# A four-part kernel (attention, experts, delta rule, feed-forward): attention's maxima taken in pairs on TensorE's row halves, and the query and key parts moved as four-byte words

## The chip, the cores and the metric

One core of one Trainium2 chip. The metric is the device time of one execution in microseconds (us); three runs of the kernel before lie within 0.15% of each other.

## What is computed

The input x has 2048 tokens of 256 numbers. Four blocks follow each other, each as `x = x + layernorm(block(layernorm(x)))`; the change touches the first alone.

```python
# block 1: 16 heads of 16 numbers, float32
q = rope(x @ q_w.T + q_b); k = rope(x @ k_w.T + k_b); v = x @ v_w.T + v_b
probs = softmax(einsum('bhqd,bhkd->bhqk', q, k) * 16 ** -0.5)
out = einsum('bhqk,bhkd->bhqd', probs, v) @ out_w.T + out_b
# block 2: 16 experts of which 2 are chosen for each token, and a shared one
# block 3: gated delta rule, 32 value heads, a scan over 256 tokens
# block 4: feed-forward of width 1024 with quantised weights
```

## The kernel before

The phases run one behind the other, each a block of its own with a program for every engine: PE (TensorE), DVE (VectorE), ACT (ScalarE), POOL (GpSimd) and SP (the queue that issues DMAs). A phase begins when every engine has ended the one before. The order on each engine is the order in which the code is written; engines wait for each other by counters.

**Head phase** (`head_phase`, line 173). It normalises x, turns it, and projects queries and keys: 16 blocks `n` of 128 features (8 heads) by 512 tokens, in the order q, k, k, q of four blocks each (`place`). A block passes DVE (`rotate`, line 389), POOL (`put_together`), ACT (`highest`, line 350), DVE (`remainder`), ACT (`middle`) and POOL (`lowest`), and leaves three bfloat16 parts, high, middle and low, whose sum is the float32 value. SP writes the three parts of each block to DRAM (line 235, `parts_away`), and after each four blocks reads them back (line 243, `heads_back`) so that the 16 features of a head stand on partitions in six bands of 16 rows, in such an order that one product over the 96 rows adds the six part products that count. Such a load is three DMAs, of 48, 32 and 16 partitions with 32 KB each. All DMAs of SP go through one queue in order. `highest` of block n waits until the writes of block n - 3 have landed, since there are three buffers (`parts`). The values are projected last (line 323).

**Attention phase** (`attention_phase`, line 418). A step is one tile of 128 keys or queries of one head; there are 16 steps to a head, 256 in all. Softmax needs each query's maximum first:

- `maximum` (line 494) multiplies 128 queries by 512 keys with the 96 rows of the six bands, four times per step, into a ring of three PSUM banks `mx`; DVE takes the maximum of each (line 632). After a head's last step DVE splits the 16 x 128 maxima into three bfloat16 parts (`split_maxima`, lines 600 to 611), PE turns them (line 525), ACT copies them (line 580) and SP writes them as rows 96 to 98 of the query operand (line 590). The key operand has ones there, set once and copied in the head phase (lines 227 and 399), so that scores come out with the maximum taken off.
- `scores` (line 505): 99 rows, 128 keys by 512 queries, four per step, in two PSUM tiles `sc` of 1024. ACT takes the exponential of each 1024 (line 568).
- `weigh` (line 517): values by probabilities, in float32, the four blocks of queries on four groups of 32 columns of the array, into `o_ps`. A float32 matmul is two instructions in the trace.
- At a head's end ACT copies `o_ps` (line 574), PE turns it (line 534), and DVE divides (lines 620 and 623).

Scores run `LAG` = 20 steps behind the maxima. PE's order in a step is mx, two scores, mx, two scores, mx, o_ps of the step before, mx. POOL stages each head's values (line 475).

## Time and profile before

| | us |
|---|---|
| median of three runs | 3882.52 (3880.14 to 3885.17) |
| the profiled execution | 3883.3 |
| its span, first to last instruction | 3881.6 |
| head phase | 0 to 145.3 |
| attention: maxima alone | 145.3 to 195.7 |
| attention: steps with maxima and scores | 195.7 to 888 |
| attention: scores alone | 888 to 934.9 |
| the other three blocks | 934.9 to 3881.6 |

The trace is of one execution. A row of its time line has the start, the time from the first start to the last end, the engine, the line of the code, the operation with its tiles and shapes, and how many instructions it merges; in brackets the idle time before it and what ended that. PE's matmuls are pipelined and their ends are modelled, so what counts for PE is the distance between starts. PEld is the load of a matmul's weights, SPq an issue on SP's queue, PEq the sequencer of PE.

### The profile page before, as it was taken

What the parts mean: (1) busy time and instruction counts of PE and PEld (TensorE: products, weight loads), DVE (VectorE), ACT (ScalarE), POOL (GpSimd) and SP (SyncE); (2) the same over time, 40 slices, a digit from 0 to 9 for tenths busy, and PEclk for the clock granted to TensorE, in tenths of its full rate; (3) what the DMA queues carried; (4) which work ended last, traced back from release to release, by engine and by line L of the source; (5) the groups of instructions that cost most, each with busy time, mean ns of one, the idle gap of its engine ahead of it and who ended that gap; (6) DMA issues with size and microseconds to landing.
All of it is one profiled execution on the core that took longest, in us unless ns stands there. A gap on an engine that the chain in (4) does not pass through costs nothing. (4 is left out here: it accounts for less than half of the span.)

```text
span 3881.6 us, 69297 instructions
## 1 busy us (share of the span) xinstructions
PE 3555.1 (92%) x22894; PEld 2220.9 (57%) x22894; DVE 2831.3 (73%) x6720; ACT 2428.1 (63%) x6502; POOL 1926.0 (50%) x4662
## 2 busy tenths in 40 slices
PE   6699999998896379999999999999999999999789
PEld 3133333333553247777777777777777777777645
DVE  4688888883423368888888888888888888888543
ACT  1066666666232367777777777777777777777411
POOL 3100000001302267877777777777777787777300
PEclk9599999999898589999999999999999999999999
DMA  6500000003222111111111110111111111111010
GB/s 162 95 1 1 1 1 1 1 1 128 96 81 86 34 27 30 39 33 30 40 34 28 41 41 21 40 41 29 32 41 31 38 33 41 30 36 25 16 37 17
DMA packets 201619, 149.25 MB, mean 38 GB/s; under 512 B 148740, under 2 KB 185732, under 8 KB 197681
## 3 DMA queue, kind: packets, MB, share of 16 engines
q1 hardware_dynamic: 198192, 136.42, 13.7%
q0 software_dynamic: 3072, 8.39, 0.7%
q8 instruction: 187, 3.06, 0.3%
q14 instruction: 168, 1.37, 0.1%
HBM read 102.69 MB, written 41.68 MB: 37 GB/s over the span
## 5 line engine op out<-in xcount | busy, mean ns | idle before, releaser
L2260 POOL TENSOR_TENSOR dl_blocks_tmp<-dl_blocks_l,dl_blocks_x 128x60 f32<-128x60 f32 (+24 forms) x1984 | 713.1, 359 | 307.4 <-DMA dl_blocks_l<-lm_dram 171.4
L2265 POOL TENSOR_TENSOR dl_blocks_x<-dl_blocks_x,dl_blocks_tmp 128x60 f32<-128x60 f32 (+24 forms) x1984 | 701.7, 354 | 155.4
L632 DVE TENSOR_REDUCE part_max<-mx 128x1 f32<-128x512 f32 x1024 | 637.0, 683 | 81.4 <-PE mx L494 81.3
L568 ACT ACTIVATE normed_t<-sc 128x1024 f32<-128x1024 f32 x512 | 496.4, 1021 | 222.1 <-PE sc L505 221.9
L2417 DVE SCALAR_TENSOR_TENSOR dl_conv<-dl_raw,dl_weights,dl_conv 128x512 f32<-128x512 f32 x768 | 580.7, 784 | 28.5 <-ACT dl_conv L2188 23.9
L1959 PE MATMUL prep<-normed_t,dl_weights 128*128 128x512 f32 x1024 | 484.2, 596 | 18.7 <-DMA dl_weights<-in_w_delta 17.3
L494 PE MATMUL mx<-k_t,q_t 96*128 96x512 bf16 x1024 | 375.0, 401 | 23.9 <-PEq L182 15.1
L475 POOL COPY v_staged<-v 128x256 f32<-128x256 f32 x16 | 6.3, 400 | 704.6 <-PE o_ps L517 704.6
L2118 ACT ACTIVATE dl_q_state<-rec_a,t_neg_decay 128x128 f32<-128x128 f32 x512 | 160.4, 366 | 239.4 <-DVE dl_r L2322 239.4
L505 PE MATMUL sc<-q_t,k_t 99*128 99x512 bf16 x1024 | 305.5, 381 | 0.6
L2128 ACT ACTIVATE dl_v<-rec_b,dl_s 128x128 f32<-128x128 f32 x512 | 164.9, 385 | 175.8 <-DVE dl_v L2330 97.2
L517 PE MATMUL o_ps<-normed_t,v_staged 128*32 128x512 f32 x2048 | 272.7, 605 | 0.4 <-ACT normed_t L568 0.4
L2064 PE MATMUL gate_y_ps<-dl_weights,dl_gated_t 128*128 128x256 f32 x1024 | 271.7, 388 | 0.9 <-ACT dl_gated_t L2133 0.9
L494 PEld LDWEIGHTS mx<-k_t,q_t 96*128 96x128 bf16 x1024 | 82.8, 97 | 324.3 <-DVE part_max L632 253.8
L2330 DVE TENSOR_TENSOR dl_v<-rec_b,dl_s_decayed 128x256 f32<-128x256 f32 x256 | 108.7, 425 | 213.6 <-PE rec_b L2037 204.7
L1959 PEld LDWEIGHTS prep<-normed_t,dl_weights 128*128 128x128 f32 x1024 | 176.7, 192 | 148.0 <-issue 144.3
L1973 PE MATMUL prep<-dl_weights,normed_t 128*128 128x256 f32 x1024 | 249.5, 387 | 0.0
L2289 POOL TENSOR_TENSOR dl_out_scale<-dl_out_scale,t_mhalf 128x2 f32<-128x2 f32 x256 | 185.9, 726 | 82.3 <-ACT dl_out_scale L2143 65.6
L2187 ACT ACTIVATE dl_raw<-prep 128x512 f32<-128x512 f32 x256 | 153.1, 598 | 102.4 <-PE prep L1959 102.3
L2322 DVE SCALAR_TENSOR_TENSOR dl_r<-rec_a,t_neg_decay,dl_v_scaled 128x128 f32<-128x128 f32 x512 | 155.2, 344 | 83.2 <-PE rec_a L2028 81.2
L2338 DVE SCALAR_TENSOR_TENSOR dl_state<-dl_state,t_chunk_decay,rec_a 128x128 f32<-128x128 f32 x512 | 153.8, 341 | 71.7 <-PE rec_a L2044 69.7
L1973 PEld LDWEIGHTS prep<-dl_weights,normed_t 128*128 128x128 f32 x1024 | 185.2, 191 | 22.6
(306 smaller groups left out, 7810.0 us busy)
## 6 DMA issues: line engine op xcount, KB each, us to landing
dl_blocks_l<-lm_dram SPq DMA_DIRECT2D x256, 128.0 KB, 2.7
dl_weights<-in_w_delta SPq DMA_DIRECT2D x16, 1032.0 KB, 4.9
lm_dram<-dl_lm SPq DMA_DIRECT2D x256, 32.0 KB, 1.7
xs_dram<-dl_blocks_x SPq DMA_DIRECT2D x64, 128.0 KB, 2.5
dl_inverse_t<-xs_dram SPq DMA_DIRECT2D x256, 32.0 KB
qk_dram<-hd_parts SPq DMA_DIRECT2D x48, 128.0 KB
rows_dram<-moe_zeros SPq DMA_DIRECT2D x1, 6016.0 KB, 23.1
moe_x_rows<-rows_dram SPq DMA_DIRECT2D x47, 128.0 KB, 2.2
```

The costliest lines, as they stand in the source:

```text
L494: pe.matmul(bank_of(x)[:, :], QT[0:SPLIT_ROWS, i, qt * P:(qt + 1) * P], KT[0:SPLIT_ROWS, i, b * 512:(b + 1) * 512], start=True, stop=True) ...
L505: last = pe.matmul(sc[u][:, b, :], KT[0:SCORE_ROWS, h, kt * P:(kt + 1) * P], QT[0:SCORE_ROWS, h, (2 * u + b) * BQ:(2 * u + b + 1) * BQ], s ...
L517: last = pe.matmul(o_ps[32 * qb:32 * qb + 32, :], vs[h % 2][:, kt, :], probs[:, kt % 2, qb * BQ:(qb + 1) * BQ], start=(kt == 0), stop=(kt ...
L568: act.activation(probs[:, e % 2, u * 2 * BQ:(u + 1) * 2 * BQ], flat(sc[u][:, :, :]), ACT.Exp, scale=float(DH) ** -0.5).then_inc(s["exp_don ...
L632: dve.reduce_max(part_max[:, t % NT, x[2]:x[2] + 1], bank_of(x)[:, :], AX.X).then_inc(s["ring_read"], 1)
L1959: last = pe.matmul(flat(bank[:, :, :]), proj_w(kh, k, m, 1), x_cols(k, q, 0, QT_), start=(k == 0), stop=(k == KD - 1))
L1973: last = pe.matmul(flat(PB[1 + u][:, 2 * j:2 * j + 2, :]), x_cols(k, q, (2 * u + j) * P, P), proj_w(kh, k, CH, VH), start=(k == 0), stop=( ...
L2064: last = pe.matmul(gy[:, 1, :], gt[g % 2][:, h, :], w_out(kh)[:, h, :], start=(h == 0), stop=(h == VH - 1))
L2260: pool.tensor_tensor(out, L[:, 0:i, i].unsqueeze(1).broadcast_to([P, NM - c0, i]), Xs[:, c0:NM, i:i + 1].broadcast_to([P, NM - c0, i]), AL ...
L2265: pool.tensor_tensor(Xs[:, c0:NM, 0:i], Xs[:, c0:NM, 0:i], out, ALU.add).then_inc(s["solve_step"], 1)
L2289: pool.tensor_tensor(osc[g % 2][:, :], osc[g % 2][:, :], tab["mhalf"], ALU.pow).then_inc(s["root_done"], 1)
L2417: dve.scalar_tensor_tensor(cv[:, m, :], raw[:, m, k:k + QT_], tap(kh, m, k), cv[:, m, :], ALU.mult, ALU.add).then_inc(s["conv_step"], 1)
```

## The change

The layout of the six bands depends on the head's parity. An even head's operands stand on rows 0 to 95 with its maxima on rows 96 to 98; an odd head's bands are turned by 64 rows, to 64 to 127 and 32 to 63, with the maxima on rows 0 to 2 and zeros on 3 to 31. The four products that matter for a maximum now fill rows 0 to 63 of an even head and rows 64 to 127 of an odd one. In each step but the first and last eight, the two matmuls of a pair belong to neighbouring heads, the upper half of one's query tiles beside the lower half of the next one's; they write the two banks of one `mx` tile, which DVE reduces in one instruction. Both pairs of a step stand between scores two and three. The scores have three PSUM tiles of 512 and ACT takes exponentials of 512. The ring has two slots of two banks, the lag is 28 steps.

The parts go through DRAM as float32 words of two bfloat16 numbers; a load comes in six pieces (q) or eight (k) instead of three, for even and odd heads apart. The ones and zeros are set by POOL at the start of attention instead of by DVE and a DMA in the head phase.

On PE, some steps into attention; `mx0` to `mx2` and `sc0` to `sc2` are PSUM tiles, `o_ps` the weighted values. Before:

```order
L494 MATMUL mx2<-k_t,q_t 128x512
L494 MATMUL mx0<-k_t,q_t 128x512
L505 MATMUL sc0<-q_t,k_t 128x512 x2
L494 MATMUL mx1<-k_t,q_t 128x512
L505 MATMUL sc1<-q_t,k_t 128x512 x2
L494 MATMUL mx2<-k_t,q_t 128x512
L517 MATMUL o_ps<-normed_t,v_staged0 32x512 x4
```

The same place now:

```order
L557 MATMUL sc0<-q_t,k_t 128x512
L557 MATMUL sc1<-q_t,k_t 128x512
L545 MATMUL mx1<-k_t,q_t 128x512 x2
L545 MATMUL mx0<-k_t,q_t 128x512 x2
L557 MATMUL sc2<-q_t,k_t 128x512
L557 MATMUL sc0<-q_t,k_t 128x512
L569 MATMUL o_ps<-normed_t,v_staged0 32x512 x4
```

The four mx matmuls, which stood apart between the scores, stand together as two pairs, with scores on both sides.

On SP in the head phase, from the first part writes to the third load; `hd_parts` are the parts, `q_t` and `k_t` the operands. Before:

```order
L235 DMA qk_dram<-hd_parts 8x16x512 x15
L243 DMA q_t<-qk_dram 48x16384
L243 DMA q_t<-qk_dram 32x16384
L243 DMA q_t<-qk_dram 16x16384
L235 DMA qk_dram<-hd_parts 8x16x512 x12
L243 DMA k_t<-qk_dram 48x16384
L243 DMA k_t<-qk_dram 32x16384
L243 DMA k_t<-qk_dram 16x16384
L235 DMA qk_dram<-hd_parts 8x16x512 x12
```

And now:

```order
L238 DMA qk_dram<-hd_parts 8x16x256 x15
L250 DMA q_t<-qk_dram 32x4096 x6
L238 DMA qk_dram<-hd_parts 8x16x256 x12
L250 DMA k_t<-qk_dram 32x4096
L250 DMA k_t<-qk_dram 16x4096 x2
L250 DMA k_t<-qk_dram 32x4096 x2
L250 DMA k_t<-qk_dram 16x4096 x2
L250 DMA k_t<-qk_dram 32x4096
L238 DMA qk_dram<-hd_parts 8x16x256 x12
```

The places of the loads between the writes are the same; each load is six or eight issues of half the bytes per partition and at most 32 partitions.

```diff
+def place_of(h):
+    return h // 8 * 8 + h % 8 // 2 + h % 2 * 4
...
-    PART_AT = ((0, 1, 2), (2, 1, 0))
+    PART_AT = ((1, 2, 0), (1, 0, 2))
+    BANDS = (((0, 2, slice(1, 3)), (32, 2, slice(1, 3)), (64, 2, slice(0, 2))),
+             ((0, 2, slice(0, 2)), (32, 1, slice(1, 2)), (48, 1, slice(0, 1)), (64, 2, slice(1, 3))))
...
-            sp.wait_ge(s["one_set"], 1)
-            sp.dma_start(KT[SPLIT_ROWS:SCORE_ROWS, 1:HEADS, :],
-                         KT[SPLIT_ROWS:SCORE_ROWS, 0:1, :].broadcast_to([MAX_ROWS, HEADS - 1, T])
-                         ).then_inc(s["ones_in"], 16)
...
-                    sp.dma_start(a["qk_dram"][side, u, part, :, :, BT * b:BT * b + BT].rearrange("d h t -> h d t"),
-                                 parts[n % DEEP][:, part, :]).then_inc(parts_out[n % DEEP], 16)
+                    sp.dma_start(a["qk_dram"][side, u, part, :, :, BW * b:BW * b + BW].rearrange("d h t -> h d t"),
+                                 parts[n % DEEP][:, part, :].bitcast(F32)).then_inc(parts_out[n % DEEP], 16)
...
-                for band, first, n in ((0, 0, 3), (3, side, 2), (5, 2 * side, 1)):
-                    sp.dma_start(flat((QT, KT)[side][DH * band:DH * (band + n), HALF * u:HALF * u + HALF, :]),
-                                 a["qk_dram"][side, u, first:first + n, :, :, :].rearrange("c d h t -> (c d) (h t)")
-                                 ).then_inc(heads_in[u], 16)
+                for odd in range(2):
+                    for row, band, chosen in BANDS[side]:
+                        at = (row + 64 * odd) % P if row < 64 else 64 - 32 * odd
+                        quarter = slice(HALF // 2 * odd, HALF // 2 * (odd + 1))
+                        to = slice(HALF * u + quarter.start, HALF * u + quarter.stop)
+                        sp.dma_start((QT, KT)[side][at:at + DH * band, to, :].rearrange("p h t -> p (h t)").bitcast(F32),
+                                     a["qk_dram"][side, u, chosen, :, quarter, :].rearrange("c d h t -> (c d) (h t)")
+                                     ).then_inc(heads_in[u], 16)
...
-            dve.memset(KT[SPLIT_ROWS:SCORE_ROWS, 0, :], 1.0).then_inc(s["one_set"], 1)
...
-    LAG = NT + 4
-    RING = 3
+    HALF = NT // 2
+    LAG = NT + HALF + 4
+    RING = 2
+    LEAD = SPLIT_ROWS - 2 * DH
...
-        mx = [c.ps(ctx, f"mx{i}", [P, 512]) for i in range(RING)]
-        sc = [c.ps(ctx, f"sc{i}", [P, 2, 512]) for i in range(2)]
+        mx = [c.ps(ctx, f"mx{i}", [P, 2, 512]) for i in range(RING)]
+        sc = [c.ps(ctx, f"sc{i}", [P, 512]) for i in range(3)]
...
+        def pair(t, v):
+            if t < HALF or t >= STEPS - HALF:
+                h, q = (0, t) if t < HALF else (HEADS - 1, t - STEPS + NT)
+                return [(h, q, 2 * v), (h, q, 2 * v + 1)]
+            h, j = divmod(t - HALF, NT)
+            b = 2 * (j % 2) + v
+            return sorted([(h, HALF + j // 2, b), (h + 1, j // 2, b)], key=lambda x: x[0] % 2)
...
+            for h in range(HEADS):
+                if h % 2:
+                    pool.memset(QT[0:2 * DH, place_of(h), :], 0.0).then_inc(s["rows_set"], 1)
...
+                    pool.memset(KT[0:2 * DH, place_of(h), :], 0.0).then_inc(s["rows_set"], 1)
...
+                pool.memset(KT[at:at + MAX_ROWS, place_of(h), :], 1.0).then_inc(s["rows_set"], 1)
...
-                pe.matmul(bank_of(x)[:, :], QT[0:SPLIT_ROWS, i, qt * P:(qt + 1) * P],
-                          KT[0:SPLIT_ROWS, i, b * 512:(b + 1) * 512], start=True, stop=True
-                          ).then_inc(s["ring_filled"], 1)
+                for i, (h, q, b) in enumerate(pair(t, v)):
+                    at = 64 * (h % 2)
+                    last = pe.matmul(bank_of(x)[:, i, :], QT[at:at + LEAD, place_of(h), q * P:(q + 1) * P],
+                                     KT[at:at + LEAD, place_of(h), b * 512:(b + 1) * 512], start=True, stop=True)
+                last.then_inc(s["ring_filled"], 1)
...
-                if e:
-                    pe.wait_ge(s["exp_done"], 2 * (e - 1) + u + 1)
...
+                    pe.wait_ge(s["rows_set"], rows_set_by(h))
+                if n >= 3:
+                    pe.wait_ge(s["exp_done"], n - 2)
...
             for t in range(LAST):
                 e = t - LAG
+                if 0 <= e < STEPS:
+                    scores(e, 0)
+                    scores(e, 1)
                 if t < STEPS:
                     maximum(t, 0)
...
                     maximum(t, 1)
                 if 0 <= e < STEPS:
-                    scores(e, 1)
...
+                    scores(e, 2)
+                    scores(e, 3)
                 if 0 <= e - 1 < STEPS:
                     weigh(e - 1)
...
-                        dve.reduce_max(part_max[:, t % NT, x[2]:x[2] + 1], bank_of(x)[:, :], AX.X
-                                       ).then_inc(s["ring_read"], 1)
+                        low, high = ((h % 2) * NT * QB + q * QB + b for h, q, b in pair(t, x[2]))
+                        dve.tensor_reduce(flat(part_max[:, :, :, :])[:, low:high + 1:high - low], bank_of(x)[:, :, :],
+                                          AX.X, ALU.max).then_inc(s["ring_read"], 1)
...
-    aps["qk_dram"] = nc.dram_tensor("qk_dram", (2, 2, 3, DH, HEADS // 2, T), BF16).ap()
+    aps["qk_dram"] = nc.dram_tensor("qk_dram", (2, 2, 3, DH, HEADS // 2, T // 2), F32).ap()
```

The weights' columns are sorted to match `place_of` on the host side of the program's layout; the projections themselves, the values among them, are as before.

## Rows read from the trace of the kernel before

**Rows 1.** Busy us of each engine by stage, granted clock, DMA share.

```profile
core 0: us, PE busy (x) PEld busy (x) DVE busy (x) ACT busy (x) POOL busy (x), PEclk, DMA share, GB/s
145.30:195.70 50.40, 48.80 (x85) 8.97 (x86) 49.49 (x88) 0.27 (x1) 1.61 (x6) 0.50 0.35 53
195.70:888.00 692.30, 682.19 (x3835) 209.35 (x3832) 608.50 (x1055) 468.62 (x500) 5.60 (x14) 1.00 0.01 1
```

**Rows 2.** Time line of PE, a steady step: start, us, engine line op.

```profile
600.50 0.60 PE L494 MATMUL mx<-k_t,q_t 96*128 96x512 bf16 x2
600.94 0.60 PE L505 MATMUL sc<-q_t,k_t 99*128 99x512 bf16 x2
...
602.03 0.38 PE L494 MATMUL mx<-k_t,q_t 96*128 96x512 bf16 x1
602.34 1.06 PE L517 MATMUL o_ps<-normed_t,v_staged 128*32 128x512 f32 x8
603.34 0.39 PE L494 MATMUL mx<-k_t,q_t 96*128 96x512 bf16 x1
```

**Rows 3.** The same step, DVE and ACT; in brackets, idle time before.

```profile
600.93 2.48 DVE L632 TENSOR_REDUCE part_max<-mx 128x1 f32<-128x512 f32 x4 [0.35 <-PE mx L494]
601.58 1.94 ACT L568 ACTIVATE normed_t<-sc 128x1024 f32<-128x1024 f32 x2 [0.90 <-PE sc L505]
```

**Rows 4.** Time line of PE in the delta phase: matmuls on 32-row groups.

```profile
2513.26 0.69 PE L1994 MATMUL merge_ps<-dl_inverse_t,dl_lm 32*32 32x32 f32 x32
```

**Rows 5.** Time lines of PE, expert phase, narrow windows: 128 and 48 rows.

```profile
1032.49 0.38 PE L1050 MATMUL moe_y_ps<-moe_w_down,moe_hidden_t 128*128 128x256 f32 x1
1032.71 0.79 PE L1050 MATMUL moe_y_ps<-moe_w_down,moe_hidden_t 128*128 128x256 f32 x2
1033.02 0.70 PE L1050 MATMUL moe_y_ps<-moe_w_down,moe_hidden_t 48*128 48x256 f32 x2
1033.34 0.38 PE L1050 MATMUL moe_y_ps<-moe_w_down,moe_hidden_t 48*128 48x256 f32 x1
1033.64 0.56 PE L1019 MATMUL moe_gu_ps<-moe_w_gate_up,normed_t 128*128 128x352 f32 x1
```

**Rows 6.** DVE's reductions: one line's least/median/most ns; time line of the fill.

```profile
L632 DVE TENSOR_REDUCE part_max<-mx x1024: 671/681/694, 146.0 to 888.8; 128x1 f32<-128x512 f32 x171
145.97 38.35 DVE L632 TENSOR_REDUCE part_max<-mx 128x1 f32<-128x512 f32 x64 [0.52 <-PE mx L494]
184.36 0.22 DVE L600 TENSOR_REDUCE neg_max<-part_max 128x16 f32<-128x64 f32 x1
146.72 0.10 PEld L494 LDWEIGHTS mx<-k_t,q_t 96*128 96x128 bf16 x1 [0.84 <-DVE part_max L632]
```

**Rows 7.** ACT's copy of 128 x 512 out of PSUM: least/median/most ns.

```profile
L574 ACT ACTIVATE out_sb<-o_ps x16: 597/598/604, 245.4 to 932.6; 128x512 f32<-128x512 f32 x16
```

**Rows 8.** Time line of ACT in the tail: two steps.

```profile
927.51 3.90 ACT L568 ACTIVATE normed_t<-sc 128x1024 f32<-128x1024 f32 x4 [0.27 <-PE sc L505]
```

**Rows 9.** Head phase: issues, ACT, PE; DMA issues xcount, KB, median us to landing.

```profile
45.89 1.28 SPq L243 DMA_DIRECT2D q_t<-qk_dram  x3
71.18 0.63 ACT L350 ACTIVATE hd_parts<-q_t 128x512 bf16<-128x512 f32 x1 [21.25 <-DMA qk_dram<-hd_parts]
145.35 39.64 PE L494 MATMUL mx<-k_t,q_t 96*128 96x512 bf16 x67 [15.10 <-PEq L182]
q_t<-qk_dram SPq DMA_DIRECT2D x1, 1536.0 KB, 14.0
q_t<-qk_dram SPq DMA_DIRECT2D x1, 1024.0 KB, 19.9
q_t<-qk_dram SPq DMA_DIRECT2D x1, 512.0 KB, 22.5
q_t<-max_t SPq DMA_DIRECT2D x3, 4.0 KB, 1.7
```

**Rows 10.** Time line of DVE at the start: a memset of three rows.

```profile
1.28 1.76 DVE L399 MEMSET k_t<- 3x2048 bf16 x1 [1.28 <-PEq L2594]
```

More of the change, by code:

```diff
@@ L353, in middle @@
                 act.wait_ge(s["rest_done"], n + 1)
-                act.activation(parts[n % DEEP][:, 1, :], rest[n % 2], ACT.Copy).then_inc(s["mid_done"], 1)
+                act.activation(parts[n % DEEP][:, PART_AT[place(n)[1]][1], :], rest[n % 2], ACT.Copy).then_inc(s["mid_done"], 1)
             for n in range(BLOCKS_QK + 1):
@@ L441, in attention_phase, with score_rows, max_row, rows_set_by @@
             "pad_set", "v_staged_sem", "ring_filled", "ring_read", "sc_done", "exp_done", "pv_done", "max_step",
-            "parts_ready", "max_copied", "rows_in", "o_copied", "rden_done")}
+            "parts_ready", "max_copied", "rows_in", "o_copied", "rden_done", "rows_set")}
         block = ctx.enter_context(nc.Block())
+        def score_rows(h):
+            return slice(0, SCORE_ROWS if h % 2 == 0 else P)
+        def max_row(h):
+            return SPLIT_ROWS if h % 2 == 0 else 0
+        def rows_set_by(h):
+            return sum(3 if i % 2 else 1 for i in range(h + 1))
+        def pair(t, v):
[5 more added lines that the diff above has]
+            return sorted([(h, HALF + j // 2, b), (h + 1, j // 2, b)], key=lambda x: x[0] % 2)
+        def ended(t):
+            h, j = divmod(t - HALF, NT)
+            return h - 1 if j == 0 and 1 <= h <= HEADS else None
         def fills(t):
             e = t - LAG
-            out = [("max", t, b) for b in range(QB)] if t < STEPS else []
-            if t % NT == 0 and 1 <= t // NT <= HEADS:
-                out.append(("rows", t // NT - 1, 0))
+            out = [("max", t, v) for v in range(2)] if t < STEPS else []
+            if ended(t) is not None:
+                out.append(("rows", ended(t), 0))
             if e % NT == 1 and 1 <= e // NT <= HEADS:
@@ L471, in _ @@
                 pool.wait_ge(s["pad_set"], 2 * i + 2)
+            n = 0
             for h in range(HEADS):
-                if h >= 2:
-                    pool.wait_ge(s["pv_done"], NT * (h - 1))
+                if h % 2:
+                    pool.memset(QT[0:2 * DH, place_of(h), :], 0.0).then_inc(s["rows_set"], 1)
+                    pool.wait_ge(s["rows_set"], n + 1)
+                    pool.memset(KT[0:2 * DH, place_of(h), :], 0.0).then_inc(s["rows_set"], 1)
+                    pool.wait_ge(s["rows_set"], n + 2)
+                at = max_row(h)
+                pool.memset(KT[at:at + MAX_ROWS, place_of(h), :], 1.0).then_inc(s["rows_set"], 1)
+                n = rows_set_by(h)
+                pool.wait_ge(s["rows_set"], n)
+                if h < 2:
+                    pool.tensor_copy(vs[h][:, :, 0:DH], V[:, :, h, :]).then_inc(s["v_staged_sem"], 1)
+                    pool.wait_ge(s["v_staged_sem"], h + 1)
+            for h in range(2, HEADS):
+                pool.wait_ge(s["pv_done"], NT * (h - 1))
                 pool.tensor_copy(vs[h % 2][:, :, 0:DH], V[:, :, h, :]).then_inc(s["v_staged_sem"], 1)
@@ L498, in scores @@
             def scores(e, u):
                 h, kt = divmod(e, NT)
+                n = QB * e + u
                 if kt == 0 and u == 0:
                     pe.wait_ge(s["rows_in"], 16 * MAX_ROWS * (h + 1))
-                if e:
-                    pe.wait_ge(s["exp_done"], 2 * (e - 1) + u + 1)
-                for b in range(2):
-                    last = pe.matmul(sc[u][:, b, :], KT[0:SCORE_ROWS, h, kt * P:(kt + 1) * P],
-                                     QT[0:SCORE_ROWS, h, (2 * u + b) * BQ:(2 * u + b + 1) * BQ], start=True, stop=True)
@@ L507, in scores @@
-                last.then_inc(s["sc_done"], 1)
+                    pe.wait_ge(s["rows_set"], rows_set_by(h))
+                if n >= 3:
+                    pe.wait_ge(s["exp_done"], n - 2)
+                pe.matmul(sc[n % 3][:, :], KT[score_rows(h), place_of(h), kt * P:(kt + 1) * P],
+                          QT[score_rows(h), place_of(h), u * BQ:(u + 1) * BQ], start=True, stop=True
+                          ).then_inc(s["sc_done"], 1)
             def weigh(e):
                 h, kt = divmod(e, NT)
-                pe.wait_ge(s["exp_done"], 2 * e + 2)
+                pe.wait_ge(s["exp_done"], QB * e + QB)
@@ L586, in _ @@
                 sp.wait_ge(s["max_copied"], h + 1)
+                sp.wait_ge(s["rows_set"], rows_set_by(h))
                 for part in range(MAX_ROWS):
-                    row = SPLIT_ROWS + part
-                    dst = QT[row:row + 1, h:h + 1, :].rearrange("r a (t c) -> r (a t) c", t=NT)
+                    row = max_row(h) + part
+                    dst = QT[row:row + 1, place_of(h):place_of(h) + 1, :].rearrange("r a (t c) -> r (a t) c", t=NT)
                     sp.dma_start(dst, max_t[part * NT:(part + 1) * NT, :]).then_inc(s["rows_in"], 16)
@@ L2540, in layout @@
         for n in "qk":
-            for order in (np.arange(D), swapped):
+            for order in (by_head.reshape(D), by_head[..., ::-1, :].reshape(D)):
                 pick = order[P * u:P * u + P]
```

57 lines of the change are left out of this document (27 added, 30 removed).

## The prediction

> **What bounds the kernel now.** I read the busy times by stage first [rows 1]. The change touches only the first two phases, which take 934.9 of the 3881.6 us; the 2946.7 us behind them run the same instructions and are taken as they are. Inside attention there are four pieces. From 145.3 to 195.7 there are maxima alone, and DVE is busy 49.5 of 50.4 us while TensorE has its half clock (0.50). From 195.7 to 888 a step repeats in which PE is busy 682 of 692 us, DVE 609, ACT 469. The tail after 888 has scores without maxima: PE and ACT only. Before 145.3 lies the head phase.
>
> A steady step [rows 2] runs from 600.50 to 603.34, that is 2.84 us: eight bfloat16 matmuls that start 0.22 us apart (two from 600.50 to 600.94), then the eight o_ps instructions, which need 1.00 us (602.34 to 603.34), and an excess of 0.09 before them, since the last mx starts at 602.03 and o_ps only at 602.34, 0.31 later. PE is never idle there. DVE waits 0.35 us in each step and ACT 0.90 [rows 3]; so PE sets the step, with DVE close behind.
>
> **The change, part by part. Maxima on row halves.** Four mx matmuls become two pairs, each pair one matmul on rows 0 to 63 and one on rows 64 to 127. If the halves work at the same time, a pair costs one slot of 0.22 us and the step loses two slots, 0.44 us. That parts of the array do work at once shows in o_ps: eight instructions that take about 0.6 us each need 1.00 us together [rows 2]. For row groups the nearest row is a run in the delta phase whose 32 small matmuls alternate between rows 0 to 31 and 64 to 95 and all lie within 0.69 us [rows 4], 0.02 each.
>
> Against this stands the price of going to half the array and back. In the expert phase the same thing happens between 128-row and 48-row matmuls [rows 5]: starts 1032.49 and 1032.71 are 0.22 apart, the first 48-row one comes 0.31 later (1033.02), the next 0.32, and the first full-height one again 0.30 (1033.64). So a change costs 0.09 us, and where the weights are float32 another 0.10 in the slot behind it, because they load only after the change. Bfloat16 weights after a change cost almost nothing extra: mx behind o_ps in rows 2 has its neighbour 0.22 to 0.23 later, so I take 0.01. The Trainium skill, TensorEngine Tiling (Array Packing), section Tiling Modes, says that changing the tiling mode drains the engine; the 0.09 us of rows 5 agrees. That rule speaks against the change: taken alone, its two added drains give back nearly half of what the pairs save.
>
> Before, a step had two changes (into and out of o_ps). Now it has four, since the pairs stand between two scores on either side. New step: four scores 4 x 0.22, two pairs 2 x 0.23, o_ps 1.00 with 0.09 before it, two more changes 2 x 0.10, in all 2.62 us by unrounded starts (0.217 for a slot).
>
> **Does anything else end later than 2.62?** DVE: back to back a reduction of 512 takes 0.599 us (38.35 us for 64) and one of 64 elements 0.22 against 0.68 [rows 6], so 512 more elements cost 0.53 and a reduction of a pair takes 1.13, two of them 2.26 per step. But the ring now has two slots instead of three: the second pair of a step waits for the second reduction of the step before. First pair's start to the reduction's start 0.43 (rows 2 and 3), first reduction 1.13, second 1.21 until its end, 0.06 to PE (the first reduction, 145.97, ends 0.69 later, and the weights that wait for its slot load at 146.72): 2.83 after the first pair's start; PE comes there by itself at 2.62 + 0.23 = 2.85. It fits, with 0.02 us to spare. ACT: an exponential of 512 takes 0.60 [rows 7]; two of 1024 take 1.94 together, so one starts 0.92 after another and half the size 0.50: four need 2.0 us, up from 1.84, below 2.62. They are covered by PE, except in the tail.
>
> **Fill, steps and tail.** The lag grows from 20 to 28 steps. Fill: 50.4 us before; now 28 x 2.26 plus 1.2 for the first split of the maxima (184.36 to 185.53), 64.9 with the start: +14.5. Steps with both: before 236 x 2.84 = 670. Now 220 x 2.62, and the last eight steps pair two blocks of the same head, on the same half, one behind the other: 8 x 3.05. Together 601: -69. Tail: two steps take 4.17 us (3.90 + 0.27) [rows 8], 20 of them 41.7. Now a step cannot be faster than this chain: a score to its exponential 0.42, the exponential 0.60, to PE 0.06, the fourth score to o_ps 0.31, o_ps 1.00: 2.39. The fourth score waits because there are three score banks. 28 x 2.39 = 66.9: +25. Head boundaries keep their instructions, but a transposed row of maxima now holds one slot of two; I take 0.25 us for each of 16 heads, +4 (bounds 0 and one pair's reduction each, 18). Attention: +14.5 - 69 + 25 + 4 = **-25.5 us**.
>
> **Head phase.** Three of its four loads of heads lie on the path: ACT stands still for 21.25 us after the first [rows 9] because the part writes queue behind the load, and attention starts (first mx at 145.35, after 15.1 us of waiting) only when the last load has been issued. A load takes 23.4 us from its first issue to its last landing (22.5 and two issues of 0.43). Its middle piece, 1024 KB on 32 partitions, lands 6.3 us after the one before (19.9 + 0.43 - 14.0), and the last, 512 KB on 16 partitions, 3.0 after that. So 512 KB on 32 partitions need 3.15. A q load becomes six such: 18.9 and 1.7 of start (the landing time of the 4 KB rows). A k load becomes four such and four of 256 KB on 16 partitions at 1.5: 18.6 and 1.7. That is -3 for each of three loads, -9; the last load's issue takes three more issues of 0.43, +1.3. **-8 us.** The upper bound is the pace of the 48-partition piece (12.3 us for 1536 KB): 26.3 per load, so +10 in all; the lower one is half of ACT's stall in two loads, -21. The width of the words changes no byte: I give it nothing. The Trainium skill, SBUF — State Buffer, section Door 1: The DMA port swizzle, says that 32 partitions reach 8 of 16 ports and 16 partitions 4, at some 27 GB/s each. By that page a q load would be 14.4 us and a k load 19.2 plus the start, and the head phase an estimated -11; no row here shows ports, so it does not enter the sum.
>
> **Work on other queues.** POOL gets 32 memsets of up to 32 x 2048; the DVE memset of 3 x 2048 that goes away took 1.76 us [rows 10], so about 56 us, on an engine that did 16 copies in all of attention. Behind them queue the value copies from the third head on, which PE needs some 150 us after the start; PE's first scores wait for one memset, SP's rows for the same counter. Cost nothing; if they took twice as long, still nothing. The removed copy of ones and its wait were early and off the path: nothing.
>
> **Sum.** The profiled execution took 3883.3 us (span 3881.6; the median of the runs is 3882.5). 3883.3 - 25.5 - 8 = 3849.8, so **3850 us**, 0.8% faster.
>
> **Rivals.**
> 1. *DVE takes the step over.* If the reduction of a pair costs two of 512 (2 x 0.60), the ring chain is 0.43 + 1.20 + 1.28 + 0.06 = 2.97, against 2.85: half of the 0.12 enters each step, because the delay also moves the next first pair. Step 2.69, +15, and the fill +4: 3869. Against it: rows 6 give the slope. For: the margin is 0.02.
> 2. *The loads do not shorten,* or the doubled number of pieces eats it: +10 instead of -8, 3868.
> 3. *Slower: changing to half the array costs more here.* A change may wait for the matmul's recorded end (0.38 - 0.22 = 0.16) and load its weights uncovered (0.10 in rows 5, float32). Then the two new changes cost 0.26 each, the step is 2.94, and 3850 becomes 220 x 0.32 + 8 x 0.32 = 73 us more: 3923. It turns slower than before where a change costs over 0.17, for then 228 steps give back the 33 us. For it: rows 5 are float32 and no row has this change with bfloat16. Against it: 0.09 at each of four changes in rows 2 and 5.
> 4. *The halves do not overlap* and the change does not do what it says: four slots and two more changes, 3.05 a step, 3944. Rows 4 and o_ps speak against it.
>
> **How the numbers follow.** Forecast 0.60 (3838 to 3862; a few in a hundred lower still, by the loads), rival 1 0.15, rival 2 0.10, rival 3 0.12, rival 4 0.03. The range reaches down to 3828 for the loads and up to 3885 over rivals 1 and 2 with a part of their spread; rivals 3 and 4 stay out. A measurement of this kernel tells 0.2% (8 us) from no change. Faster: the forecast and most of rivals 1 and 2, 0.77; same 0.09; slower 0.14.
>
> **What would show it.** Right: steps of 2.62 us with the two mx of a pair starting within 0.01; 0.31 between a score and the first mx and between the last mx and a score; pair reductions of 1.2 us; first exponential 65 us after the first mx; tail steps of 2.39; first mx near 137. Wrong: mx of one pair 0.22 apart (rival 4), gaps of 0.4 or more at the changes (rival 3), PE waiting for DVE in each step (rival 1), first mx at 145 or later (rival 2).

## The result and the profile after

| | us |
|---|---|
| before, median of 4 runs | 3883.85 (3880.14 to 3890.03) |
| after, median of 4 runs | 3860.01 (3856.19 to 3861.15) |
| ratio, 95% interval | 0.9936 (0.9924 to 0.9948) |
| after, the profiled execution and its span | 3856.2, 3854.5 |
| forecast, and its range | 3850 (3828 to 3885) |

The kernel became 0.6% faster; the forecast was 0.8%. The busy times by stage of the kernel after, cut at the first mx, the first exponential, the last mx and the first matmul of the next block (the first two lines of attention answer to [rows 1]):

```profile
core 0: us, PE busy (x) PEld busy (x) DVE busy (x) ACT busy (x) POOL busy (x), PEclk, DMA share, GB/s
140.95:209.62 68.67, 41.33 (x115) 6.56 (x115) 66.78 (x63) 0.27 (x1) 59.08 (x38) 0.50 0.18 39
209.62:836.54 626.92, 606.75 (x3664) 138.28 (x3698) 559.52 (x568) 501.16 (x938) 5.61 (x14) 0.99 0.01 1
836.54:909.97 73.43, 63.36 (x362) 14.42 (x364) 4.79 (x12) 60.53 (x118) 0.04 (x1) 1.00 0.00 1
```

Cut at the same four events, the stages of before are 145.35, 50.39, 692.67, 46.64 and 2946.52 us. So the head phase is 4.4 shorter, the fill 18.3 longer, the stretch of steps 65.8 shorter, the tail 26.8 longer, and what is behind attention 2.0 shorter with the same instructions: 27.1 us less between the two profiled executions. In the fourteen profiles of this study that last part took 2941 to 2950 us, so some 4 us of any single time come from there and not from the change. The profiled execution (3856.2) is the lowest of the four; it lies below the median (3860.0) by about as much, but where the others lost that is not known, since one execution was traced.

A steady step on PE, time line, then the same step on DVE and ACT (they answer to [rows 2] and [rows 3]):

```profile
600.31 0.60 PE L557 MATMUL sc<-q_t,k_t 99*128 99x512 bf16 x2
600.85 0.63 PE L545 MATMUL mx<-k_t,q_t 64*128 64x512 bf16 x4
601.41 0.60 PE L557 MATMUL sc<-q_t,k_t 99*128 99x512 bf16 x2
601.95 1.06 PE L569 MATMUL o_ps<-normed_t,v_staged 128*32 128x512 f32 x8
602.94 0.61 PE L557 MATMUL sc<-q_t,k_t 99*128 99x512 bf16 x2
```

```profile
601.28 2.36 DVE L684 TENSOR_REDUCE part_max<-mx 128x2 f32<-128x1024 f32 x2 [0.25 <-PE mx L545]
600.74 2.18 ACT L618 ACTIVATE normed_t<-sc 128x512 f32<-128x512 f32 x4 [0.45 <-PE sc L557]
```

A step is 602.94 - 600.31 = 2.63 us. The four mx stand in one row: the first pair starts at 600.85, and the next score 0.56 later, where four slots and a change would have needed 0.97. The two matmuls of a pair start 0.003 us apart throughout the stretch. The first mx comes 0.31 after the second score (600.54), as a first 48-row matmul came 0.31 after a 128-row one [rows 5]. DVE waits 0.25 us in a step, ACT 0.45, PE not at all.

DVE in the fill, and POOL at its end (they answer to [rows 6] and [rows 10]):

```profile
142.00 55.01 DVE L684 TENSOR_REDUCE part_max<-mx 128x2 f32<-128x1024 f32 x48 [0.94 <-PE mx L545]
197.30 1.21 DVE L657 CAST max_parts<-neg_max 128x16 bf16<-128x16 f32 x1
198.76 1.61 DVE L657 CAST max_parts<-neg_max 128x16 bf16<-128x16 f32 x1
200.61 1.61 DVE L662 CAST max_parts<-neg_max 128x16 bf16<-128x16 f32 x1
203.75 9.20 DVE L684 TENSOR_REDUCE part_max<-mx 128x2 f32<-128x1024 f32 x8 [0.71 <-PE mx L545]
```

```profile
196.69 1.79 POOL L510 MEMSET q_t<- 32x2048 bf16 x1
198.54 1.79 POOL L512 MEMSET k_t<- 32x2048 bf16 x1
200.39 1.79 POOL L515 MEMSET k_t<- 3x2048 bf16 x1
```

48 pair reductions take 55.01 us, 1.146 each (1.131 from the seventeenth on). Then the three casts that split the first head's maxima take 1.21, 1.61 and 1.61 us, though the same operations take 0.17 at every later head; each of them ends 0.03 us behind the end of a memset on POOL (198.48, 200.33, 202.18). The last line shows DVE waiting 0.71 us soon after, while PE turns the split maxima.

The head phase: ACT's two stops, SP's last load, the first mx (they answer to [rows 9]):

```profile
66.40 0.63 ACT L356 ACTIVATE hd_parts<-q_t 128x512 bf16<-128x512 f32 x1 [16.16 <-DMA qk_dram<-hd_parts]
100.15 0.63 ACT L356 ACTIVATE hd_parts<-q_t 128x512 bf16<-128x512 f32 x1 [21.70 <-DMA qk_dram<-hd_parts]
137.81 2.69 SPq L250 DMA_DIRECT2D q_t<-qk_dram  x6
140.95 1.44 PE L545 MATMUL mx<-k_t,q_t 64*128 64x512 bf16 x3 [14.67 <-PEq L190]
```

The tail, PE and ACT (they answer to [rows 8]): three scores, then a wait for ACT, then the fourth score and o_ps, 2.40 us from step to step.

```profile
838.38 0.82 PE L557 MATMUL sc<-q_t,k_t 99*128 99x512 bf16 x3
839.46 0.39 PE L557 MATMUL sc<-q_t,k_t 99*128 99x512 bf16 x1 [0.26 <-ACT normed_t L618]
841.20 2.06 ACT L618 ACTIVATE normed_t<-sc 128x512 f32<-128x512 f32 x4 [0.33 <-PE sc L557]
```

### The profile page after: what moved, and what is told of

Same layout as the page of the kernel before. It is cut to its first block and busy times, and to the rows that moved or that the text cites. A ratio compares the mean times of both kernels' runs of the same rounds, so it can differ in the third digit from the quotient of the medians.

```text
span 3854.5 us, 69321 instructions
## 1 busy us (share of the span) xinstructions
PE 3493.7 (91%) x22855; PEld 2153.0 (56%) x22894; DVE 2799.5 (73%) x6207; ACT 2480.4 (64%) x7014; POOL 1989.5 (52%) x4694
## 5 line engine op out<-in xcount | busy, mean ns | idle before, releaser
L684 DVE TENSOR_REDUCE part_max<-mx 128x2 f32<-128x1024 f32 x512 | 601.7, 1222 | 65.5 <-PE mx L545 64.7
L618 ACT ACTIVATE normed_t<-sc 128x512 f32<-128x512 f32 x1024 | 550.4, 596 | 127.6 <-PE sc L557 126.5
L557 PE MATMUL sc<-q_t,k_t 99*128 99x512 bf16 (+1 forms) x985 | 302.7, 386 | 12.6 <-ACT normed_t L618 8.1
L545 PE MATMUL mx<-k_t,q_t 64*128 64x512 bf16 x1024 | 187.3, 410 | 46.1 <-DVE part_max L684 25.1
L557 PEld LDWEIGHTS sc<-q_t,k_t 128*128 128x128 bf16 (+1 forms) x1024 | 63.9, 98 | 275.5 <-ACT normed_t L618 251.9
```

The costliest lines, as they stand in the source:

```text
L545: last = pe.matmul(bank_of(x)[:, i, :], QT[at:at + LEAD, place_of(h), q * P:(q + 1) * P], KT[at:at + LEAD, place_of(h), b * 512:(b + 1) * ...
L557: pe.matmul(sc[n % 3][:, :], KT[score_rows(h), place_of(h), kt * P:(kt + 1) * P], QT[score_rows(h), place_of(h), u * BQ:(u + 1) * BQ], sta ...
L618: act.activation(probs[:, e % 2, u * BQ:(u + 1) * BQ], sc[n % 3][:, :], ACT.Exp, scale=float(DH) ** -0.5).then_inc(s["exp_done"], 1)
L684: dve.tensor_reduce(flat(part_max[:, :, :, :])[:, low:high + 1:high - low], bank_of(x)[:, :, :], AX.X, ALU.max).then_inc(s["ring_read"], 1)
```

## The experiments

| label | what | median us | ratio to before, 95% interval |
|---|---|---|---|
| e1_late | memsets out of the fill | 3855.4 | 0.9925 (0.9911 to 0.9938) |
| e2_k32 | key loads of 32 rows, outer count 2 | 3909.8 | 1.0070 (1.0056 to 1.0083) |
| e3_bf16 | words of bfloat16 | 3858.8 | 0.9937 (0.9923 to 0.9950) |
| e4_tail | six banks in the tail | 3845.4 | 0.9903 (0.9888 to 0.9918) |
| e5_onehalf | pairs on one half | 3947.8 | one run |
| e6_full | maxima on all 96 rows | 3896.2 | one run |
| e7_apart | pairs apart | 3895.3 | one run |
| e8_quarter | memsets in four pieces | 3856.5 | one run |
| e9_k32b | key loads of 32 rows, outer count 16 | 3848.1 | 0.9911 (0.9896 to 0.9926) |
| e10_lag27 | lag 27 | 3856.9 | 0.9929 (0.9915 to 0.9943) |
| e11_combined | e1, e4 and e10 | 3842.9 | 0.9896 (0.9881 to 0.9911) |
| e12_all | e11 and e9 | 3832.0 | 0.9861 (0.9845 to 0.9878) |

All are edits of the kernel after.

### The step: overlap, and the price of a change

Three edits. **e5_onehalf** puts both matmuls of a pair on the same half of the rows:

```diff
-                    at = 64 * (h % 2)
+                    at, h = 0, h - h % 2
```

> Both matmuls of every pair take rows 0 to 63 (the odd head's maxima are replaced by the even head's, so the odd heads' outputs are another computation; the work and its order are the same). Theory: halves overlap, so one half alone costs two slots more per step: 2.62 + 2 x 0.22 = 3.06 us a step, 220 x 0.43 = 95 us more, 3955. Rival: the overlap is not what saves (the 64-row matmuls are simply cheaper): the step stays near 2.62, 3860.

PE's time line in e5_onehalf, one step and the start of the next:

```profile
641.86 0.60 PE L557 MATMUL sc<-q_t,k_t 99*128 99x512 bf16 x2
642.40 1.03 PE L545 MATMUL mx<-k_t,q_t 64*128 64x512 bf16 x4
643.37 0.60 PE L557 MATMUL sc<-q_t,k_t 99*128 99x512 bf16 x2
...
644.90 0.60 PE L557 MATMUL sc<-q_t,k_t 99*128 99x512 bf16 x2
```

The step is 644.90 - 641.86 = 3.04 us (median of all steps 3.037, against 2.629). The four mx take 0.97 until the next score, where they took 0.56, and the two of a pair start 0.22 us apart instead of 0.003. So a pair on two halves saves 0.204 us: nearly a whole slot of 0.217.

**e6_full** takes all 96 rows for the maxima, as before the change, but in the order and with the reductions of after:

```diff
+                    at, h = 0, h - h % 2
-                    last = pe.matmul(bank_of(x)[:, i, :], QT[at:at + LEAD, ...
+                    last = pe.matmul(bank_of(x)[:, i, :], QT[at:at + SPLIT_ROWS, ...
```

> The maxima's matmuls take all 96 rows, in the changed kernel's order and with its paired reductions (the odd head's maxima are again replaced by the even head's). No mode change at the pairs and no overlap. Theory: 8 x 0.217 + 1.00 + 0.09 = 2.83 us a step, as before the change: 220 x 0.21 less 8 x 0.20 in the last steps is 45 us more, 3905. If the new order or the paired reductions gave the gain instead, the step stays at 2.62 and the time at 3860.

The same view of e6_full:

```profile
650.14 0.60 PE L557 MATMUL sc<-q_t,k_t 128*128 128x512 bf16 x2
650.58 1.03 PE L545 MATMUL mx<-k_t,q_t 96*128 96x512 bf16 x4
651.45 0.60 PE L557 MATMUL sc<-q_t,k_t 128*128 128x512 bf16 x2
...
652.97 0.61 PE L557 MATMUL sc<-q_t,k_t 128*128 128x512 bf16 x2
```

652.97 - 650.14 is 2.83 us (median 2.833; before the change 2.837). The mx start 0.44 after the scores, two slots, and the next scores 0.87 after the mx, four slots: no change between them costs anything. So in the step the new order, the paired reductions and the ring of two gave nothing; its whole gain is the halves. The time, 3896.2, is 9 us below what was expected: beside the profiled execution of after (3856.2) it is 40 more, of which the stretch of steps has 39.6, the fill 2.7 and the head phase 1.2, and the blocks behind attention, short in this run, take 3.4 back.

**e7_apart** stands the pairs apart, score, pair, two scores, pair, score: two changes more.

```diff
                     scores(e, 0)
-                    scores(e, 1)
                 if t < STEPS:
                     maximum(t, 0)
+                if 0 <= e < STEPS:
+                    scores(e, 1)
+                    scores(e, 2)
+                if t < STEPS:
                     maximum(t, 1)
                 if 0 <= e < STEPS:
-                    scores(e, 2)
                     scores(e, 3)
```

> The two pairs of a step stand apart: score, pair, two scores, pair, score. That adds two mode changes to each step and nothing else. Theory: a change costs 0.10 us, so the step goes from 2.62 to 2.82 and the time up by 220 x 0.2 = 44 us, 3904. Rival: a change costs 0.26, step 3.14, 3974. Or none at all (the drain hides): 2.62, 3860.

The same view of e7_apart:

```profile
641.67 0.39 PE L557 MATMUL sc<-q_t,k_t 128*128 128x512 bf16 x1
641.99 0.39 PE L545 MATMUL mx<-k_t,q_t 64*128 64x512 bf16 x2
642.31 0.60 PE L557 MATMUL sc<-q_t,k_t 128*128 128x512 bf16 x2
...
644.49 0.39 PE L557 MATMUL sc<-q_t,k_t 128*128 128x512 bf16 x1
```

Each time the kind of row group changes, the next start is 0.32 behind the last one instead of 0.22 (641.67 to 641.99 to 642.31). The step is 2.82 (median 2.822), so a change costs (2.822 - 2.629) / 2 = 0.097 us with bfloat16 operands. With that the step of after follows: 2.833 less two overlaps of 0.204 plus two changes of 0.097 is 2.62. With each pair between scores, as the old order had the maxima, almost nothing of the step would have been gained (2.82 against 2.84).

All three times came 7 to 9 us below what was expected of them. None of the expectations counted the head boundary, the time that a head takes beyond its sixteen steps: 1.72 us in the kernel after, but 1.03 in e5_onehalf, 1.55 in e6_full and 1.25 in e7_apart (DVE's splits stand 43.78, 49.62, 46.88 and 46.40 us apart). Over some fifteen boundaries that is 10, 3 and 7 us; on top come the fill and the 4 us by which single executions differ. What sets the boundary was not followed.

### The fill: POOL's memsets and DVE's casts

**e1_late** sets the fixed rows of heads 0 to 3 at the start and those of the others one by one, behind the value copies:

```diff
-            for h in range(HEADS):
+            for h in range(4):
+                fixed_rows(h)
...
             for h in range(2, HEADS):
                 pool.wait_ge(s["pv_done"], NT * (h - 1))
                 pool.tensor_copy(...)
+                if h + 2 < HEADS:
+                    pool.wait_ge(s["v_staged_sem"], h + 1)
+                    fixed_rows(h + 2)
```

> The memsets of heads 4 to 15 on POOL move out of the fill, each behind the value copy of the head two before it. Theory: in the changed kernel each of the first split's three casts on DVE (1.21, 1.61, 1.61 us) ended with a POOL memset because the two engines share something; without memsets there the casts take 0.17 as in every later split, the fill falls from 68.7 to 64.8 us, and the time by 3.9, to 3856. Rival: the first casts are slow for a reason of their own (they are the first of their kind): they stay at 1.2 to 1.6 and the time stays at 3860.

The time line of e1_late at the end of the first split, the last cast on DVE and then PE:

```profile
198.47 0.17 DVE L667 CAST max_parts<-neg_max 128x16 bf16<-128x16 f32 x1
199.82 0.33 PE L582 MATMUL mx<-identb,max_parts 128*80 128x128 bf16 x1 [1.81 <-DVE part_max L689]
```

All three casts take 0.17. The fill is 66.19 instead of 68.67 us: 2.5 less and not 3.9, since PE now waits for a slot of the ring: it turns the rows at 199.82 (last row), 1.18 after the last cast, where it turned them 0.14 after it in the kernel after. The median is 3855.4; its interval overlaps with that of after, so it is the stage that shows the gain, not the time.

**e8_quarter** keeps the memsets where they are and cuts each into four:

```diff
+                def fill(what, value, n):
+                    for i in range(4):
+                        pool.memset(what[:, 512 * i:512 * i + 512], value).then_inc(s["rows_set"], 1)
+                    pool.wait_ge(s["rows_set"], n + 4)
...
-                    pool.memset(QT[0:2 * DH, place_of(h), :], 0.0).then_inc(s["rows_set"], 1)
...
+                    fill(QT[0:2 * DH, place_of(h), :], 0.0, n)
```

> Every memset of POOL's fixed rows is cut into four of 512 columns; the amount of work is the same. Theory: a cast of the first split waits until the memset that runs has ended, so its wait is at most a quarter memset, some 0.45 to 0.5 us: the three casts take at most 0.7 each instead of 1.21, 1.61, 1.61, and the fill falls by 2.4 to 3.4 us. Rival: the casts share a port's pace with POOL over their whole length: they stay at 1.2 to 1.6.

The same casts on DVE's time line in e8_quarter:

```profile
198.11 0.38 DVE L661 CAST max_parts<-neg_max 128x16 bf16<-128x16 f32 x1
198.74 0.25 DVE L661 CAST max_parts<-neg_max 128x16 bf16<-128x16 f32 x1
199.23 0.24 DVE L666 CAST max_parts<-neg_max 128x16 bf16<-128x16 f32 x1
```

0.38, 0.25 and 0.24: between the 0.17 of no memset and the 1.61 of whole ones, as a wait for the end of the piece that is running would give. POOL filled the same bytes, so it isn't the amount that slows the casts. The fill is 2.2 us shorter than in the kernel after (66.46), a little less than the 2.4 to 3.4 expected: PE waits for its slot of the ring here too. The reductions beside the memsets did not change (1.131 us from one to the next from the seventeenth on, with whole memsets, quarters or none). The Trainium skill, SBUF — State Buffer, section Who interferes with whom, says that a cast on VectorE can take the port pair that it shares with GpSimd, that whoever holds it keeps it for a whole instruction while the other is blocked, and that a tensor_reduce on trn2 doesn't use it. These rows agree in each of the three points.

### The loads of the head phase

**e3_bf16** undoes the width of the words alone:

```diff
-                                 parts[n % DEEP][:, part, :].bitcast(F32)).then_inc(...)
+                                 parts[n % DEEP][:, part, :]).then_inc(...)
...
-    aps["qk_dram"] = nc.dram_tensor("qk_dram", (2, 2, 3, DH, HEADS // 2, T // 2), F32).ap()
+    aps["qk_dram"] = nc.dram_tensor("qk_dram", (2, 2, 3, DH, HEADS // 2, T), BF16).ap()
```

> The parts go through DRAM as bfloat16 again, with the same pieces. Theory: the width of the words moves no byte more or less, so the loads, the stops of ACT (16.2 and 21.7 us) and the time, 3860, stay within 2 us. Rival: the words of four bytes shortened the query load, and it goes back from 16.2 to 21 us: 3865.

3858.8 us; ACT's stops are 16.06 and 21.02 us, the first mx at 140.56 (after: 16.16, 21.70, 140.95). The width does nothing. What shortened the query load, from its first issue to ACT's next work, from 25.3 (71.18 - 45.89) to 20.2 us (66.40 - 46.20), is then the pieces; their number, their size and their rows changed together and were not told apart.

Why did the key loads not follow? The page of DMA traffic of the kernel after, two stretches of the first key load: from 78 to 81, when its pieces on 16 partitions move, and from 84 to 87, when pieces on 32 do.

```profile
DMA packets 35, 0.31 MB, mean 104 GB/s; under 512 B 16, under 2 KB 16, under 8 KB 16
DMA packets 55, 0.64 MB, mean 213 GB/s; under 512 B 16, under 2 KB 16, under 8 KB 16
```

104 GB/s in the one, 213 in the other (other windows of 2 or 3 us over the 16-row pieces, some with the end of a neighbour, gave 87 to 131). **e2_k32** does away with the 16-row pieces: the order of the parts is changed, and a piece of 32 rows reads one part twice, by a source that repeats.

```diff
-    PART_AT = ((1, 2, 0), (1, 0, 2))
+    PART_AT = ((1, 2, 0), (0, 2, 1))
...
-             ((0, 2, slice(0, 2)), (32, 1, slice(1, 2)), (48, 1, slice(0, 1)), (64, 2, slice(1, 3))))
+             ((0, 2, 0), (32, 2, 2), (64, 2, slice(0, 2))))
...
+                            src = a["qk_dram"][side, u, chosen:chosen + 1, :, quarter, :].rearrange("c d h t -> c d (h t)")
+                            sp.dma_start(dst, src.broadcast_to([band, DH, HALF // 2 * BW * GROUPS])
```

> A key load comes in six pieces of 512 KB on 32 partitions instead of eight, four of them 256 KB on 16 partitions (the order of the parts and of the six bands is changed so that no 16-row piece is left). Theory: the 16-row pieces run at half the pace (their packets of 16 KB take 2.3 to 2.8 us against 1.27 in the 32-row pieces); a key load then takes what a query load takes, ACT's second stop falls from 21.7 to about 16.2 us, the last load starts some 5 earlier again, and the time falls by 10, to 3850. Rival: key loads are slow for another reason (traffic, their place in the queue): only two issues of 0.43 us per load go away, 2 us in all, 3858.

ACT's time line in e2_k32 at its second stop, and then the lines on DMA packets from 94 to 97 us (the second has their number, MB and share of the time of 16 engines):

```profile
126.14 0.63 ACT L361 ACTIVATE hd_parts<-q_t 128x512 bf16<-128x512 f32 x1 [48.04 <-DMA qk_dram<-hd_parts]
```

```profile
DMA packets 10, 0.16 MB, mean 55 GB/s; under 512 B 0, under 2 KB 0, under 8 KB 0
q1 hardware_dynamic: 10, 0.16, 12.8%
```

Neither theory: ACT's second stop grew to 48 us. The traffic from 94 to 97 us is ten packets of 16 KB in 3 us. The source is now [2, 16, 4096] with the repetition outside. A packet took 0.61 us in that stretch, so ten in 3 us are two at a time, and 12.8% of sixteen engines is two: two DMA engines work and the others don't. **e9_k32b** changes that order: 16 features outside, two parts inside, for queries and keys.

```diff
-    a["qk_dram"][side, u, chosen, :, quarter, :].rearrange("c d h t -> (c d) (h t)")
+    a["qk_dram"][side, u, chosen, :, quarter, :].rearrange("c d h t -> d c (h t)")
+    .broadcast_to([DH, band, HALF // 2 * BW * GROUPS])
```

> As the run before with key loads in six pieces of 512 KB on 32 partitions, but the rows of a piece are ordered feature by feature (16 features outside, two parts inside), for queries too, so that the outer count of the source is 16 and not 2. Theory: the run before was slow (+50 us) because a source whose outer count is 2 went to two DMA engines at a time (about ten packets of 0.61 us in 3 us); with 16 outside all engines work again, and without 16-row pieces a key load takes what a query load takes: ACT's second stop 16 instead of 21.7 us, the last load starts another 5 earlier, 10 us less than the changed kernel, 3850. Rival: it was the source with repeated rows itself that is slow: above 3900 again. Second rival: key loads are not slow by their 16-row pieces: the second stop stays at 21, the time at 3858.

The time lines of ACT and SP in e9_k32b, and then the line on DMA packets from 78 to 81 us:

```profile
94.21 0.63 ACT L357 ACTIVATE hd_parts<-q_t 128x512 bf16<-128x512 f32 x1 [15.79 <-DMA qk_dram<-hd_parts]
126.17 3.77 SPq L250 DMA_DIRECT2D q_t<-qk_dram  x6
```

```profile
DMA packets 55, 0.61 MB, mean 202 GB/s; under 512 B 18, under 2 KB 18, under 8 KB 18
```

ACT's second stop is 15.79 us, as after a query load; the last load starts at 126.17 instead of 137.81; the rate from 78 to 81 is 202 GB/s, and the same page has the engines busy for 96.2%. From its first issue to that of the next load a key load takes 27.85 and 23.96 us, where it took 33.75 and 29.66: 5.9 and 5.7 less, while the query load did not change (28.21 against 28.20). The time is 3848.1, 12 below that of the kernel after (the intervals, 0.9911 and 0.9936 of before, meet only at their ends). So the 16-row pieces were what held the key loads, and the order of the source's counts what held e2. The Trainium skill has both: SBUF — State Buffer, section Door 1: The DMA port swizzle, gives 16 partitions half the ports of 32, some 109 and 218 GB/s, and the 104 and the 202 to 213 of these loads agree; DMA: Bandwidth & Descriptors, section Why a DMA increments its semaphore by 16 and not by 1, says that the number of engines is the largest up to 16 that divides the outermost counts of both sides, and e2's two (12.8%) and e9's sixteen (96.2%) agree.

### The tail, the lag, and all together

**e4_tail** lets the scores of the tail use the banks of the ring, which has no maxima left:

```diff
+        spare = [mx[1][:, 0, :], mx[1][:, 1, :], mx[0][:, 1, :]]
+        tail_banks = [sc[(FREE + i) % 3][:, :] for i in range(3)] + spare
+        def score_bank(n):
+            return sc[n % 3][:, :] if n < FREE else tail_banks[(n - FREE) % 6]
```

> In the tail, where there are no maxima, the scores take turns in six PSUM banks instead of three. Theory: a tail step of 2.39 us is a chain (the fourth score waits for the first exponential's bank); with banks enough it is bound by PE, 4 x 0.22 + 1.00 + 0.19 = 2.06, or by four exponentials, 2.05: 28 steps x 0.32 = 9 us less, 3851. Rival: o_ps and the two buffers of the probabilities set the 2.39 and nothing moves: 3860.

PE's time line in e4_tail, a step of the tail:

```profile
871.99 1.07 PE L583 MATMUL o_ps<-normed_t,v_staged 128*32 128x512 f32 x8
872.99 0.82 PE L571 MATMUL sc<-q_t,k_t 128*128 128x512 bf16 x3
...
873.96 1.07 PE L583 MATMUL o_ps<-normed_t,v_staged 128*32 128x512 f32 x8
```

873.96 - 871.99 = 1.97 us a step, with PE never waiting: four scores and o_ps in 4 x 0.22 + 1.00 and one change. (The expectation counted the change behind o_ps twice: it is in the 1.00.) From DVE's last reduction to the next block the kernel takes 59.4 us instead of 71.1. The time is 3845.4, 14.6 below after, of which the stage shows 11.7.

**e10_lag27** changes `LAG` from `NT + HALF + 4` to `NT + HALF + 3`.

> The scores run 27 instead of 28 steps behind the maxima. Theory: a step of lag costs a step of the fill (2.26) and one of the tail (2.40) less one with both (2.63), 2.0 us, and the rows of maxima land 4.7 us before their first score, so a step less brings no wait: 3858 from 3860. Rival: the rows come late and each of 15 heads waits: 3860 or more.

3856.9 us. The fill is 2.23 shorter, the tail 2.4, the stretch of steps 1.1 longer: 3.5 by the stages, where 2.0 was expected. The time lies where it was expected, but its interval can't tell it from after.

**e11_combined** joins e1, e4 and e10, and **e12_all** adds e9.

> Memsets out of the fill, six score banks in the tail, and a lag of 27 steps together. Theory: they act in different stages and add up: 2.5 of the fill, 28 x 0.43 = 12 and some in the tail, 2.26 + 1.97 - 2.63 = 1.6 for the lag: 16 us less than the changed kernel, 3844, and about 39 less than the kernel before. Rival: a gain in one stage is lost in the next: 3846 to 3855.

> The three changes of the run before (memsets out of the fill, six score banks in the tail, lag 27) with key loads in 32-row pieces ordered feature by feature. Theory: the loads are in the head phase and the rest in attention, so the gains add: 12 less than the run before, 3831, and 53 less than the kernel before. Rival: the earlier start of attention meets something in the head phase that was hidden (the value projection, SP's queue): 3835 to 3843.

3842.9 and 3832.0 us. The gains add, for each lies in a stage of its own: in e11_combined attention is 16.2 us shorter than in after (fill 4.7, steps and tail together 11.5), as expected. The head phase in front of it took 143.32 us instead of 140.95 with the same instructions, and it is as long in e12_all (132.91 against 130.64 in e9_k32b). 1.7 to 1.8 us of that is there when the first load is issued (48.03 against 46.20, 47.82 against 46.16); where it is from was not followed.

This last version, e12_all, is 1.4% faster than the kernel before (0.9861, 0.9845 to 0.9878), where the change alone gave 0.6%.

## Why the prediction was right, and where not

The time lay 10 us above the forecast, within its range, with the sign that was forecast. By its steps:

1. **The step: right.** 2.62 was forecast, 2.63 came. Each of its terms has its own experiment: the overlap (e5_onehalf, 0.204 a pair against 0.217), the change (e7_apart, 0.097 against 0.10), no gain from the order itself (e6_full, 2.833 against 2.837 before). The price of the change was taken from float32 rows of another block, and it held for bfloat16, which no row before had shown. Rivals 3 and 4 are out by the same runs.
2. **DVE: right.** A pair reduction takes 1.131 us, as the slope of [rows 6] gave (1.13), and PE does not wait for the ring in a steady step. Rival 1 is out.
3. **Steps and boundaries: right.** -69 and +4 forecast, -65.8 measured. The last eight steps take 3.04 (3.05). A head takes 43.78 us (DVE's splits at 287.80 and 331.58), 1.72 beyond its 16 steps, where it was 1.65: 0.07 more, not the 0.25 taken for the ring of two slots.
4. **Tail: right in its mechanism.** 2.40 a step against 2.39; the stage gained 26.8 for 25. e4_tail shows that the chain through the three banks is what sets it.
5. **Fill: too small by 3.8 us.** The failed term is the one on other queues: "Cost nothing; if they took twice as long, still nothing" looked at who waits behind POOL, and not at what DVE shares with it. Whole memsets hold the casts: 2.5 us (e1_late). The fill's own term, 28 x 2.26, also left out that DVE waits 0.71 us while PE turns the first rows, and that the first 16 reductions come every 1.21 and 1.14 us in turn instead of every 1.13, 0.56 together: those pairs are on one half, one behind the other. The three make 3.8. Where all pairs are on one half (e5_onehalf) this goes on through the fill: 1.5 us more by the 48th reduction, and 1.3 at the split and behind it.
6. **Head phase: -4.4 for -8.** The first query load gave 5.1 instead of 3; the two key loads gave -0.2 and 0.8 instead of 3 each; the longer issue of the last load cost 1.0 for 1.3, and 0.3 went at the start. The failed step is the price of a piece of 256 KB on 16 partitions, 1.5 us, half of the 3.0 by which one landing follows another in [rows 9]. Such a difference is not the duration of a piece when the two overlap; their rate shows it (104 against 213 GB/s, 2.5 us for 256 KB), and e9_k32b gives the 5.7 to 5.9 us per load that the four pieces cost more than two of 512 KB. The other two prices were off as well, one each way. The profile's lines on DMA issues have the first and the last piece of the first query load of after (issued at 46.20 and 48.55):

```profile
q_t<-qk_dram SPq DMA_DIRECT2D x1, 512.0 KB, 6.7
q_t<-qk_dram SPq DMA_DIRECT2D x1, 512.0 KB, 15.9
```

The first lands 6.7 us after its issue, where 1.7 + 3.15 was forecast, and the last 11.6 us after the first, 2.3 a piece where it was 3.15. The load took 18.3 us and not 20.6; that the forecast came so near is in part luck, for the start was priced too low and the piece too high. The -4.4 is of one execution, too: in the ten traces with these loads (after, e1, e3 to e8, e10, e11) the first mx lies between 140.6 and 143.3, so the gain over the one trace of before is 2.0 to 4.8. The sentence from the Trainium skill that stood beside the sum, with its estimate of 14.4 us for a query load and 19.2 for a key load, had the order of the two right (18.3 and 23.9 by their landings) where the sum had them nearly equal, 20.6 and 20.3.

7. **Width of the words: right**, nothing (e3_bf16). Rival 2 is out for query loads; the key loads, as it said, did not shorten by much (-0.2 and 0.8).

Of the 10 us, 3.6 are the head phase, 3.8 the fill and 1.8 the tail, with -0.8 in the steps; the rest, about 2, is the difference between the profiled execution and the median (3.8) less the 2.0 by which the blocks behind attention were shorter.

## What to carry to other kernels

In this kernel two products of half the rows at once saved nearly a slot, but a change of row groups cost near half a slot: gather them so that one pair of changes serves several products, and count the changes on both sides before anything else. Cheap work that is put on an idle engine is not free when a busy neighbour has to wait for its end: ask which of the neighbour's operations do, place the work where there are none, or cut it into pieces. Read the pace of a DMA from the traffic while it runs, not from the distance of two landings, and look at how many partitions a piece has and how many rows its source counts outermost.

## What the runs showed of the hardware that was not expected

- A cast on DVE waits for a memset that runs on POOL to end: 1.21 to 1.61 us against 0.17, and 0.24 to 0.38 with memsets of a quarter; reductions out of PSUM beside the same memsets came every 1.131 us all the same.
- A DMA whose source counts two outermost ran at 55 GB/s, one with sixteen outermost, the same bytes to the same 32 rows in another order, at 202.
- Pieces on 16 partitions ran at 104 GB/s (87 to 131 in other windows) beside 202 to 213 for 32.
